# Routed expert loop: both weight blocks of a tile's expert copied at once into four buffers, and the choice of experts worked out in two parts of tiles

## Chip, cores, metric

The kernel runs on one core of one Trainium2 chip. The metric is the device time of one execution in microseconds (us). Engines are named as in the profile: PE is TensorE's matmuls, PEld its weight loads, DVE is VectorE, ACT is ScalarE, POOL is GpSimd, SP is SyncE (here only an issuer of DMAs).

## The reference, cut to what matters

The whole program is a two-layer network over x of 128 x 32 x 128 (4096 tokens of width 128). The change lies in the feed-forward part of layer 0, a mixture of 8 experts with two choices for each token:

```python
logits = x @ router_weight                  # x: 4096 x 128, 8 experts
probs = jax.nn.softmax(logits, axis=-1)
top_p, top_i = jax.lax.top_k(probs, 2)
top_p = top_p / jnp.sum(top_p, axis=-1, keepdims=True)
...                                         # an expert keeps its first cap choices, in token order
fc1 = jax.nn.gelu(jnp.einsum('ech,ehf->ecf', xt, moe_w1))      # moe_w1: 8 x 128 x 256
fc2 = jnp.einsum('ecf,efh->ech', fc1, moe_w2).reshape(T, H)    # moe_w2: 8 x 256 x 128
weighted = fc2 * padded_probs[:, None]
moe_out = jnp.zeros((N, H)).at[padded_tid].add(weighted)
return h1 + moe_out
```

The cap is 1280 choices per expert.

## The kernel before

The program is a row of stages, each with one instruction stream per engine and semaphores between them. The change touches `stage_experts_two`, which the profile shows from about 769 to 958 us. It holds 32 tiles of 128 tokens and treats them in two ways. Tiles 20 to 31 are **dense**: three blocks of four tiles, each through all 8 experts, with each expert's result added to the tokens with its share (zero if it isn't chosen). Tiles 0 to 19 are **routed**: each of their 2 x 2560 rows is stored to a row of a table in HBM that is sorted by expert, 48 tiles of 128 rows (`NS`), so that each tile has one expert.

In order, the stage does this:

1. **The choice** (DVE, lines 1848 to 1907): a chain of short instructions, each of which waits for the one before (`link`). It normalises the probabilities of all 32 tiles, finds the first and second expert (`first_of`), waits for two matmuls of PE that count the earlier tokens of each expert (`ranks`, lines 1733 and 1734), makes prefix sums over tiles, and from these the shares (`expert_shares`, semaphore `known`), the table rows of the first and second choices (`slots`, semaphore `slots_known`, one count for each choice), and the expert of each of the 48 tiles (`tile_expert`, `tiles_known`).
2. **The scatter** (POOL, line 1715): 40 indirect DMAs, one for each routed tile and choice, the first 20 after `slots_known` 1.
3. **Dense, early** (PE, ACT, DVE): meanwhile two of the three dense blocks. PE makes `h` (line 1739) and `y` (line 1749) of an expert, ACT the gelu between (line 1815), DVE adds the result (`take`, line 1924). The fourth `y` of PE waits for `known`, since its bank 7 is the one that the rank matmuls used.
4. **The routed loop** (48 tiles; the first and last 8 are written out, 32 run as four passes of a hardware loop with eight tiles in its body). SP loads a tile's rows from the table into one of 8 buffers (line 1692), and reloads a buffer when the store of its last tile's results has landed. PE transposes it (line 1767), ACT copies the transpose out of PSUM (line 1820), PE makes `slot_h` (line 1774), ACT the gelu (line 1830), PE makes `slot_y` (line 1783), DVE scales it by the token's share (`y_scale`, line 1936) into one of 4 buffers, and POOL stores it to HBM by an indirect DMA (line 1721). The tile's expert is known only in `tile_expert`, so an engine reads it into a register (`value_load`): DVE does so to copy `w1` of the expert into one of two buffers (`pick`, line 1931), PE does so to address `w2` in `slot_y`:

```python
e = pe.value_load(tile_expert[0:1, ts(t, 1)], min_val=0, max_val=E - 1)
pe.wait_ge(t_gelued, t + 1)
wait(pe, y_scaled, t - 1)
for c in range(NF):
    m = pe.matmul(pZ[slot % 2][:, 0:D], tg[slot % 2][:, c * P:(c + 1) * P],
                  w2[:, bass.ds(e * F + c * D, D)], start=(c == 0), stop=(c == NF - 1))
```

   The order on each engine is written by hand: for tile t, PE does transpose(t+1), slot_h(t), slot_y(t-1); ACT x_copy(t+1), gelu(t); DVE pick(t+1), y_scale(t-1); POOL store(t).
5. **Dense, late** on PE, ACT and DVE (the third block), during which the routed results come back from HBM and are added (`join`).

## Time and profile before

| what | value |
|---|---|
| three runs | 2177.77 us median, 2172.71 to 2177.92 |
| the profiled execution | 2173.39 us, span 2171.6 us |
| PE busy, PEld busy | 1991.1 us (92%), 1477.1 us (68%) |
| DVE, ACT, POOL busy | 1559.5, 1261.6, 1177.0 us |
| mean granted TensorE clock | 0.967 of full speed |
| this stage: the choice on DVE | 769.5 to 794.1 us |
| this stage: scatters on POOL | 792.5 to 842.9 us |
| this stage: early dense on PE | 769.5 to 834.3 us |
| this stage: routed loop on PE | 846.2 to 923.8 us |
| this stage: late dense on PE | 924.2 to 952.5 us |

Times inside the span are read from the timeline, which gives starts and durations of the instructions. The busy shares of the page are means over many stages; for this change the stretch from 769 to 924 us has to be read by itself.

### The profile page before, as it was taken

The page shows a single profiled execution, that of the slowest core. Times are in us where ns is not written, and L with a number is a line of the kernel's source. Part 1 is how long each engine was busy: PE and PEld are TensorE (multiplying, and loading weights), DVE is VectorE, ACT ScalarE, POOL GpSimd, SP SyncE. Part 2 cuts the span into 40 slices and gives each one's busy share as a digit, 9 for nine tenths or more (in the row PEclk, how much of TensorE's full clock was granted, in tenths as well). Part 3 has the DMA queues.
Part 4 walks back from the last instruction along what each step waited for, and adds up shares of the span by engine and source line. Part 5 has one row for each costly group of instructions (what it writes and reads, how often), then busy time and mean ns, then how long its engine had stood idle before and what let it go on. Part 6 is the DMA issues. An engine that isn't in the chain of part 4 may idle for free. (4 is left out here: it accounts for less than half of the span.)

```text
span 2171.6 us, 80082 instructions
## 1 busy us (share of the span) xinstructions
PE 1991.1 (92%) x26973; PEld 1477.1 (68%) x26974; DVE 1559.5 (72%) x5584; ACT 1261.6 (58%) x3636; POOL 1177.0 (54%) x1217
## 2 busy tenths in 40 slices
PE   8989999997999797869999999999789999979998
PEld 5567777774767665647777777777456666666897
DVE  6878888883777763458989898989666676654444
ACT  4555556554888533527777777777545555542332
POOL 2234433442888635636777777777266666634331
PEclk9999999997999988979999999999899999989999
DMA  6630000000000002220111111111220000000113
GB/s 216 215 126 0 0 0 0 0 1 1 1 0 0 1 20 63 81 80 26 38 36 37 37 41 39 40 36 40 95 107 0 0 0 0 0 1 29 39 49 98
DMA packets 48256, 86.63 MB, mean 40 GB/s; under 512 B 8624, under 2 KB 34224, under 8 KB 47408
## 3 DMA queue, kind: packets, MB, share of 16 engines
q1 hardware_dynamic: 43040, 74.84, 10.8%
...
## 5 line engine op out<-in xcount | busy, mean ns | idle before, releaser
L2554 ACT ACTIVATE xat_scores<-xat_scores,xat_least 128x257 f32<-128x257 f32 x512 | 258.3, 505 | 84.5 <-DVE xat_least L2695 84.5
L2695 DVE CUSTOM_DVE_ANT_0 xat_scores<-bank,xat_mask_b 128x257 f32<-128x257 f32 x512 | 202.8, 419 | 51.2 <-PE bank L2400 45.1
L1109 POOL TENSOR_TENSOR gqa_rnorm<-gqa_norm_min,gqa_minus_half 128x12 f32<-128x12 f32 x64 | 145.8, 2278 | 104.7 <-DVE gqa_norm_min L1186 104.7
L2456 PE MATMUL bank<-ident,xat_scores 128*128 128x128 f32 x1024 | 189.6, 288 | 0.2 <-DVE xat_p_T L2702 0.2
L753 POOL TENSOR_TENSOR lin_q_softmax<-lin_q_exp,lin_q_rsum 128x512 f32<-128x512 f32 x64 | 66.7, 1042 | 223.0 <-DVE lin_q_rsum L814 223.0
L2456 PEld LDWEIGHTS bank<-ident,xat_scores 128*128 128x128 f32 x1024 | 116.1, 142 | 81.8 <-issue 43.8
L1427 POOL TENSOR_TENSOR bat_scores<-bat_scores,bat_max 128x512 f32<-128x512 f32 x128 | 130.4, 1040 | 32.6 <-DVE bat_max L1459 32.6
L1459 DVE CUSTOM_DVE_ANT_0 bat_scores<-bank,bat_causal_add 128x128 f32<-128x128 f32 x512 | 110.7, 286 | 47.1 <-PE bank L1315 47.1
L631 PEld LDWEIGHTS bank<-lin_w_v_out,lin_z_T 128*128 128x128 f32 x1024 | 119.1, 191 | 22.0 <-issue 20.2
L631 PE MATMUL bank<-lin_w_v_out,lin_z_T 128*128 128x128 f32 x1024 | 131.2, 281 | 1.3 <-ACT lin_z_T L683 1.3
L2600 POOL TENSOR_TENSOR xat_p_rsum_wide<-xat_p_rsum,xat_head_of_row 128x128 f32<-128x128 f32 x128 | 51.1, 399 | 147.1 <-DVE xat_p_rsum L2708 147.1
L2567 ACT ACTIVATE xat_p_T<-bank 128x256 f32<-128x256 f32 x256 | 96.3, 377 | 49.0 <-PE bank L2456 41.5
L2702 DVE COPY xat_p_T<-bank 128x256 f32<-128x256 f32 x256 | 106.3, 415 | 0.3 <-PE bank L2456 0.2
L2400 PE MATMUL bank<-xat_k_cos,xat_q_blocks 32*128 32x257 f32 x1024 | 94.8, 431 | 7.4 <-DVE xat_least L2695 3.0
L2554 ACT ACTIVATION_READ_ACCUMULATOR xat_scores<-xat_scores,xat_least 128x1 f32 x512 | 97.5, 190 | 0.0
L1056 ACT ACTIVATE gqa_squares<-bank 128x512 f32<-128x512 f32 x64 | 38.2, 597 | 91.8 <-PE bank L919 91.7
L1382 ACT ACTIVATE bat_p_T<-bank 128x512 f32<-128x512 f32 x128 | 76.1, 594 | 24.8 <-PE bank L1323 24.8
L1323 PEld LDWEIGHTS bank<-ident,bat_scores 128*128 128x128 f32 x512 | 54.9, 142 | 50.9 <-ACT bat_scores L1377 25.3
L1323 PE MATMUL bank<-ident,bat_scores 128*128 128x128 f32 x512 | 77.4, 285 | 12.7 <-ACT bat_scores L1377 12.7
...
L704 ACT ACTIVATE lin_q_T<-bank 128x512 f32<-128x512 f32 x64 | 38.2, 597 | 79.8 <-PE bank L594 79.8
L2409 PE MATMUL bank<-xat_ctx_kept,xat_w_k 128*128 128x257 f32 x256 | 78.4, 388 | 6.4 <-POOL xat_ctx_kept L2617 6.4
...
## 6 DMA issues: line engine op xcount, KB each, us to landing
...
moe_slot_row<-moe_rows SPq DMA_DIRECT2D x48, 65.0 KB, 1.8
...
```

The lines of the kernel that those rows point to most:

```text
L631: m = pe.matmul(pY[:, 0:D], zT[slot][:, hd, :], wvo[:, hd // 2, hd % 2, :], start=(hd == 0), stop=(hd == H - 1))
L1109: pool.tensor_tensor(rn[h][:, :], sm[h][:, :], half_neg[:, :], ALU.pow).then_inc(rnorm, 1)
L1323: m = pe.transpose(pT[g % 2][:, i * P:(i + 1) * P], sx[g][:, i, :], k.ident[:, :])
L1427: pool.tensor_tensor(sx[g][:, :, :], sx[g][:, :, :], spread(mx[g][:, :], P), ALU.subtract).then_inc(s_shifted, 1)
L1459: dve.tensor_tensor_reduce(sx[g][:, i, :], pS[g][:, i * P:(i + 1) * P], cadd[:, :], 1.0, -BIG, ALU.add, ALU.max, mx[g][:, i:i + 1]).then_i ...
L2400: m = pe.matmul(pS[g][:, 0:J], qb[slot][r, part, j, :, :], keys[j % 2][r, :], start=(part == 0), stop=(part == 1))
L2409: pe.matmul(pK[:, 0:J], wk[:, :], ck[slot][:, j, :], start=True, stop=True).then_inc(k_made, 1)
L2456: m = pe.transpose(dst[:, c * P:(c + 1) * P], sx[j % 2][:, g, c * P:(c + 1) * P], k.ident[:, :])
L2554: act.activation(sx[j % 2][:, g, :], sx[j % 2][:, g, :], ACT.Exp, bias=mn[j % 2][g][:, 0:1], scale=-1.0, accum_out=sm[j % 2][:, g:g + 1]). ...
L2567: act.activation(pt[j % 2][g][:, :], unit_bank(*at)[:, 0:NC * P], ACT.Copy).then_inc(pa_copied, 1)
L2695: dve.tensor_tensor_reduce(sx[j % 2][:, g, :], pS[g][:, 0:J], mb[slot][:, j, :], 1.0, BIG, ALU.add, ALU.min, mn[j % 2][g][:, 0:1]).then_in ...
L2702: dve.tensor_copy(pt[j % 2][g][:, :], unit_bank(*at)[:, 0:NC * P]).then_inc(pd_copied, 1)
```

## The change

- `w1` and `w2` of an expert lie side by side in one array of 512 columns per expert (`wp`; one load of the same bytes instead of two).
- `pick` copies all 512 columns into one of **four** buffers, and waits for `slot_y` of three tiles before instead of `slot_h` of the last tile. `slot_y` takes `w2` from the same buffer: PE's `value_load` and its computed addresses go.
- The choice is worked out in two parts, tiles 0 to 19 (160 columns) and tiles 20 to 31 (96 columns): choose(0), share(0), choose(1), rank(0), the table rows of the first choice, share(1), rank(1), the rows of the second choice, the tiles' experts. A part has its own rank matmuls (in banks 6 and 7); a third matmul with a matrix of -1 takes the place of one subtraction on DVE. The limit and the share are made in one instruction. PE waits for `known` 1 before its third `y` and for `known` 2 before its fourth.
- `look` at the end of the stage and `LATE` are the same work written in another way.

```diff
-        we = [sb(f"picked_w1{i}", [P, F]) for i in range(2)]
+        we = [sb(f"picked_w{i}", [P, 2 * F]) for i in range(4)]
...
-        pR, pC = k.bank[7][:, 0:NT * E], k.bank[7][:, NT * E:2 * NT * E]
+        PARTS = ((0, NR), (NR, NT))
+        pR = [k.bank[6 + part][:, 0:(hi - lo) * E] for part, (lo, hi) in enumerate(PARTS)]
+        pC = [k.bank[6 + part][:, (hi - lo) * E:2 * (hi - lo) * E] for part, (lo, hi) in enumerate(PARTS)]
...
+            pool.memset(minus[:, :], -1.0).then_inc(ones_set, 1)
...
         def _(pe):
-            def ranks():
-                pe.wait_ge(ones_set, 1)
-                pe.wait_ge(sel_ready, 1)
-                pe.matmul(pR, low[:, :], sel[:, :, :], start=True, stop=True)
-                pe.matmul(pC, ones[:, :], sel[:, :, :], start=True, stop=True).then_inc(ranked, 1)
+            def ranks(part):
+                lo, hi = PARTS[part]
+                pe.wait_ge(ones_set, 2)
+                pe.wait_ge(sel_ready, part + 1)
+                pe.matmul(pR[part], low[:, :], sel[:, lo:hi, :], start=True, stop=False)
+                pe.matmul(pR[part], minus[:, :], sel[:, lo:hi, :], start=False, stop=True)
+                pe.matmul(pC[part], ones[:, :], sel[:, lo:hi, :], start=True, stop=True).then_inc(ranked, 1)
 
...
-                    pe.matmul(pH[e % 2][c][:, :], w1[:, e * F + c * P:e * F + (c + 1) * P], k.LT[:, ts(b, TB), :],
+                    pe.matmul(pH[e % 2][c][:, :], wp[:, 2 * e * F + c * P:2 * e * F + (c + 1) * P], k.LT[:, ts(b, TB), :],
...
                 pe.wait_ge(gelued, NF * n + NF)
                 wait(pe, added, TB * (n - BANKS + 1))
-                if n == BANKS - 1:
-                    pe.wait_ge(known, 1)
+                if BANKS - 2 <= n < BANKS:
+                    pe.wait_ge(known, n - BANKS + 3)
...
-                                      w2[:, (e * NF + c) * D:(e * NF + c + 1) * D], start=(c == 0), stop=(c == NF - 1))
+                                      wp[:, (2 * e + 1) * F + c * D:(2 * e + 1) * F + (c + 1) * D], start=(c == 0), stop=(c == NF - 1))
...
-                        if ranking and i == 0 and e == 2:
-                            ranks()
+                        if ranking and i == 0 and 1 <= e < 3:
+                            ranks(e - 1)
...
-                    m = pe.matmul(pT[slot % 2][:, c * P:(c + 1) * P], we[slot % 2][:, c * P:(c + 1) * P], xT[slot % 2][:, :],
+                    m = pe.matmul(pT[slot % 2][:, c * P:(c + 1) * P], we[slot % 4][:, c * P:(c + 1) * P], xT[slot % 2][:, :],
...
             def slot_y(t, slot):
-                e = pe.value_load(tile_expert[0:1, ts(t, 1)], min_val=0, max_val=E - 1)
                 pe.wait_ge(t_gelued, t + 1)
                 wait(pe, y_scaled, t - 1)
                 for c in range(NF):
                     m = pe.matmul(pZ[slot % 2][:, 0:D], tg[slot % 2][:, c * P:(c + 1) * P],
-                                  w2[:, bass.ds(e * F + c * D, D)], start=(c == 0), stop=(c == NF - 1))
+                                  we[slot % 4][:, F + c * D:F + (c + 1) * D], start=(c == 0), stop=(c == NF - 1))
                 m.then_inc(ty_made, 1)
...
+            def choose(lo, hi):
+                p, o0, o1, c = pr[:, lo:hi, :], oh[0][:, lo:hi, :], oh[1][:, lo:hi, :], k.COMB[:, lo:hi, :]
+                a, b, sums, t = top[:, lo:hi], top2[:, lo:hi], tot[:, lo:hi], tmp[:, lo:hi, :]
+                link(dve.tensor_reduce(sums, p, AX, ALU.add))
+                link(dve.reciprocal(sums, sums))
+                link(dve.tensor_tensor(p, p, spread(sums, E), ALU.mult))
+                link(dve.tensor_reduce(a, p, AX, ALU.max))
+                link(dve.tensor_copy(sums, a))
+                first_of(dve, link, t, o0, p, a, down[:, :])
+                link(dve.scalar_tensor_tensor(out=c, in0=o0, scalar=-2.0, in1=p, op0=ALU.mult, op1=ALU.add))
+                link(dve.tensor_reduce(b, c, AX, ALU.max))
+                link(dve.tensor_tensor(sums, sums, b, ALU.add))
+                first_of(dve, link, t, o1, c, b, down[:, :])
+                dve.tensor_tensor(sel[:, lo:hi, :], o0, o1, ALU.add).then_inc(sel_ready, 1)
+
+            def share(part, lo, hi):
+                dve.wait_ge(sel_ready, part + 1)
+                link(dve.reciprocal(tot[:, lo:hi], tot[:, lo:hi]))
+                link(dve.tensor_tensor(pr[:, lo:hi, :], pr[:, lo:hi, :], spread(tot[:, lo:hi], E), ALU.mult))
+                link(dve.tensor_tensor(pr[:, lo:hi, :], pr[:, lo:hi, :], sel[:, lo:hi, :], ALU.mult))
+
+            def rank(part, lo, hi, before):
+                n = hi - lo
+                dve.wait_ge(ranked, part + 1)
+                link(dve.tensor_copy(acc[0][:, lo:hi, :], pC[part].rearrange("p (t e) -> p t e", e=E)))
+                if before is not None:
+                    link(dve.tensor_tensor(acc[0][:, lo, :], acc[0][:, lo, :], before, ALU.add))
+                d, a = 1, 0
+                while d < n:
+                    link(dve.tensor_copy(acc[1 - a][:, lo:lo + d, :], acc[a][:, lo:lo + d, :]))
+                    link(dve.tensor_tensor(acc[1 - a][:, lo + d:hi, :], acc[a][:, lo + d:hi, :], acc[a][:, lo:hi - d, :],
+                                           ALU.add))
+                    d, a = 2 * d, 1 - a
+                link(dve.tensor_tensor(tmp[:, lo:hi, :], acc[a][:, lo:hi, :], pR[part].rearrange("p (t e) -> p t e", e=E),
+                                       ALU.add))
+                dve.scalar_tensor_tensor(out=k.COMB[:, lo:hi, 0:E], in0=tmp[:, lo:hi, :], scalar=float(CAP),
+                                         in1=pr[:, lo:hi, :], op0=ALU.is_lt, op1=ALU.mult).then_inc(known, 1)
+                dve.wait_ge(known, part + 1)
+                return acc[a][:, hi - 1, :]
+
+            def slot_numbers(c):
+                link(dve.tensor_tensor(picks[:, :, :], spot[:, :, :], oh[c][:, 0:NR, :], ALU.mult))
+                link(dve.tensor_reduce(spots[c][:, :], picks[:, :, :], AX, ALU.add))
+                link(dve.tensor_tensor(picks[:, :, :], k.COMB[:, 0:NR, :], oh[c][:, 0:NR, :], ALU.mult))
+                link(dve.tensor_reduce(kept[c][:, :, SHARE], picks[:, :, :], AX, ALU.add))
+                dve.tensor_copy(slots[c][:, :], spots[c][:, :]).then_inc(slots_known, 1)
...
-            link(dve.tensor_reduce(tot[:, :], pr[:, :, :], AX, ALU.add))
-            link(dve.reciprocal(tot[:, :], tot[:, :]))
...
-            first_of(dve, link, tmp[:, :, :], oh[1][:, :, :], k.COMB[:, :, :], top2[:, :], down[:, :])
-            dve.tensor_tensor(sel[:, :, :], oh[0][:, :, :], oh[1][:, :, :], ALU.add).then_inc(sel_ready, 1)
-            dve.wait_ge(sel_ready, 1)
-            link(dve.reciprocal(tot[:, :], tot[:, :]))
-            link(dve.tensor_tensor(pr[:, :, :], pr[:, :, :], spread(tot[:, :], E), ALU.mult))
-            link(dve.tensor_tensor(pr[:, :, :], pr[:, :, :], sel[:, :, :], ALU.mult))
-
-            dve.wait_ge(ranked, 1)
-            in_tile = pC.rearrange("p (t e) -> p t e", e=E)
-            link(dve.tensor_copy(acc[0][:, :, :], in_tile))
-            d, a = 1, 0
-            while d < NT:
-                link(dve.tensor_copy(acc[1 - a][:, 0:d, :], acc[a][:, 0:d, :]))
-                link(dve.tensor_tensor(acc[1 - a][:, d:, :], acc[a][:, d:, :], acc[a][:, 0:NT - d, :], ALU.add))
-                d, a = 2 * d, 1 - a
-            link(dve.tensor_tensor(tmp[:, :, :], acc[a][:, :, :], in_tile, ALU.subtract))
-            link(dve.tensor_tensor(tmp[:, :, :], tmp[:, :, :], pR.rearrange("p (t e) -> p t e", e=E),
-                                   ALU.add))
...
-            link(dve.tensor_scalar(need[:, :], acc[a][:, NR - 1, :], 1.0 / P, None, ALU.mult))
+            choose(*PARTS[0])
+            share(0, *PARTS[0])
+            choose(*PARTS[1])
+            counts = rank(0, *PARTS[0], None)
+
+            link(dve.tensor_scalar(need[:, :], counts, 1.0 / P, None, ALU.mult))
...
-            link(dve.tensor_scalar(tmp[:, :, :], tmp[:, :, :], float(CAP), None, ALU.is_lt))
-            dve.tensor_tensor(k.COMB[:, :, 0:E], pr[:, :, :], tmp[:, :, :], ALU.mult).then_inc(known, 1)
-            dve.wait_ge(known, 1)
-            for c in range(2):
-                link(dve.tensor_tensor(picks[:, :, :], spot[:, :, :], oh[c][:, 0:NR, :], ALU.mult))
-                link(dve.tensor_reduce(spots[c][:, :], picks[:, :, :], AX, ALU.add))
-                link(dve.tensor_tensor(picks[:, :, :], k.COMB[:, 0:NR, :], oh[c][:, 0:NR, :], ALU.mult))
-                link(dve.tensor_reduce(kept[c][:, :, SHARE], picks[:, :, :], AX, ALU.add))
-                dve.tensor_copy(slots[c][:, :], spots[c][:, :]).then_inc(slots_known, 1)
+            slot_numbers(0)
+            share(1, *PARTS[1])
+            rank(1, *PARTS[1], counts)
+            slot_numbers(1)
...
             def pick(t, slot):
                 e = dve.value_load(tile_expert[0:1, ts(t, 1)], min_val=0, max_val=E - 1)
-                wait(dve, th_made, t - 1)
-                dve.tensor_copy(we[slot % 2][:, :], w1[:, ts(e, F)]).then_inc(picked, 1)
+                wait(dve, ty_made, t - 3)
+                dve.tensor_copy(we[slot % 4][:, :], wp[:, bass.ds(e * 2 * F, 2 * F)]).then_inc(picked, 1)
...
-            moe_w = [eb("moe_w1", [P, 8 * 256]), eb("moe_w2", [P, 8 * 2 * D])]
+            moe_w = eb("moe_w", [P, 8 * 512])
...
+    o["moe_w"] = np.concatenate([g["L0_ffn_moe_w1"].transpose(1, 0, 2),
+                                 g["L0_ffn_moe_w2"].reshape(8, 2, P, D).transpose(2, 0, 1, 3).reshape(P, 8, -1)],
+                                axis=2).reshape(P, -1)
```

On PE, in the routed loop (written-out part, third and fourth tile; `bank` is PSUM, `moe_w` the experts' weights, `moe_picked_w` the copy of the tile's expert). Before:

```order
L1767 MATMUL bank<-ident,moe_slot_row 128x128
L1774 MATMUL bank<-moe_slot_xT,moe_picked_w 128x128 x2
L1779 TENSOR_LOAD moe_tile_expert
L1779 ISA x2
L1783 ISA
L1783 MATMUL bank<-moe_w,moe_slot_gelu 128x128
L1783 ISA
L1783 MATMUL bank<-moe_w,moe_slot_gelu 128x128
L1767 MATMUL bank<-ident,moe_slot_row 128x128
L1774 MATMUL bank<-moe_slot_xT,moe_picked_w 128x128 x2
```

With the change:

```order
L1773 MATMUL bank<-ident,moe_slot_row 128x128
L1780 MATMUL bank<-moe_slot_xT,moe_picked_w 128x128 x2
L1788 MATMUL bank<-moe_picked_w,moe_slot_gelu 128x128 x2
L1773 MATMUL bank<-ident,moe_slot_row 128x128
L1780 MATMUL bank<-moe_slot_xT,moe_picked_w 128x128 x2
L1788 MATMUL bank<-moe_picked_w,moe_slot_gelu 128x128 x2
```

The register load (TENSOR_LOAD) and the four instructions that set addresses are gone, and slot_y reads moe_picked_w.

On DVE, the same place: scaling of one tile, then the pick for the tile after the next. Before:

```order
L1936 TENSOR_SCALAR moe_slot_y<-bank,moe_slot_row 128x128
L1929 TENSOR_LOAD moe_tile_expert
L1929 ISA x2
L1931 ISA
L1931 COPY moe_picked_w<-moe_w 128x256
L1936 TENSOR_SCALAR moe_slot_y<-bank,moe_slot_row 128x128
```

With the change:

```order
L1958 TENSOR_SCALAR moe_slot_y<-bank,moe_slot_row 128x128
L1951 TENSOR_LOAD moe_tile_expert
L1951 ISA x2
L1953 ISA
L1953 COPY moe_picked_w<-moe_w 128x512
L1958 TENSOR_SCALAR moe_slot_y<-bank,moe_slot_row 128x128
```

The register load stays here; the copy has 512 columns instead of 256.

On DVE, the end of the chain that the scatter waits for, from the last prefix sum to the first choice's rows. Before:

```order
L1892 TENSOR_SCALAR moe_tokens_of<-moe_tokens_of 128x8
L1893 TENSOR_TENSOR moe_spot<-moe_tmp,moe_tokens_of 128x160
L1895 TENSOR_SCALAR moe_tmp<-moe_tmp 128x256
L1896 TENSOR_TENSOR expert_shares<-moe_probs,moe_tmp 128x256
L1899 TENSOR_TENSOR moe_picked_spot<-moe_spot,moe_onehot 128x160
L1900 TENSOR_REDUCE moe_slot_float<-moe_picked_spot 128x20
L1901 TENSOR_TENSOR moe_picked_spot<-expert_shares,moe_onehot 128x160
L1902 TENSOR_REDUCE moe_rows_kept<-moe_picked_spot 128x20
L1903 CAST moe_slot<-moe_slot_float 128x20
```

With the change, up to the beginning of the second part's prefix sums:

```order
L1919 TENSOR_SCALAR moe_tokens_of<-moe_tokens_of 128x8
L1920 TENSOR_TENSOR moe_spot<-moe_tmp,moe_tokens_of 128x160
L1894 TENSOR_TENSOR moe_picked_spot<-moe_spot,moe_onehot 128x160
L1895 TENSOR_REDUCE moe_slot_float<-moe_picked_spot 128x20
L1896 TENSOR_TENSOR moe_picked_spot<-expert_shares,moe_onehot 128x160
L1897 TENSOR_REDUCE moe_rows_kept<-moe_picked_spot 128x20
L1898 CAST moe_slot<-moe_slot_float 128x20
L1870 RECIPROCAL moe_total<-moe_total 128x12
L1871 TENSOR_TENSOR moe_probs<-moe_probs,moe_total 128x96
L1872 TENSOR_TENSOR moe_probs<-moe_probs,moe_selected 128x96
L1877 COPY moe_prefix<-bank 128x96
```

The two 256-column instructions between moe_spot and the rows are gone from here; the second part's shares and ranks stand between the first and the second choice's rows.

## Rows read from the trace of the kernel before

**Rows 1.** Waits, 800 to 960 us: engine, line, waited for; total us, times, longest.

```profile
PEld bank L1783 <- issue: 19.0, 46, 0.6
...
PE bank L1767 <- DMA moe_slot_row<-moe_rows: 11.9, 1, 11.9
```

**Rows 2.** Windows: busy us (x instructions) per engine, PEclk, DMA share, GB/s.

```profile
850.00:852.00 2.00, 2.00 (x11) 2.00 (x11) 0.70 (x2) 0.84 (x2) 0.42 (x1) 0.50 0.00 0
```

**Rows 3.** Timeline of the routed loop: start us, us, engine, line, operation, [idle before].

```profile
891.84 0.53 PEld L1774 LDWEIGHTS bank<-moe_slot_xT,moe_picked_w 128*128 128x128 f32 x4
...
892.04 0.35 DVE L1936 TENSOR_SCALAR moe_slot_y<-bank,moe_slot_row 128x128 f32<-128x128 f32 x1 [0.30 <-PE bank L1783]
...
892.84 0.71 PE L1783 MATMUL bank<-moe_w,moe_slot_gelu 128*128 x4 [0.28 <-issue]
892.89 0.29 DVE L1931 COPY moe_picked_w<-moe_w 128x256 f32 x1 [0.50 <-PE bank L1774]
893.18 0.96 POOL L1721 DMA_INDIRECT moe_results<-moe_slot_y,moe_slot_row  x1 [0.50 <-issue]
...
893.59 0.35 DVE L1936 TENSOR_SCALAR moe_slot_y<-bank,moe_slot_row 128x128 f32<-128x128 f32 x1 [0.40 <-PE bank L1783]
```

**Rows 4.** Timeline, GpSimd: first and last issue of a pass of eight, next pass.

```profile
888.70 0.96 POOL L1721 DMA_INDIRECT moe_results<-moe_slot_y,moe_slot_row  x1 [1.35 <-DVE moe_slot_y L1936]
...
899.28 0.96 POOL L1721 DMA_INDIRECT moe_results<-moe_slot_y,moe_slot_row  x1 [0.64 <-issue]
901.72 0.96 POOL L1721 DMA_INDIRECT moe_results<-moe_slot_y,moe_slot_row  x1 [1.48 <-DVE moe_slot_y L1936]
```

**Rows 5.** DMA issues, 844 to 928 us: KB each, median us from issue to landing.

```profile
moe_slot_row<-moe_rows SPq DMA_DIRECT2D x48, 65.0 KB, 1.8
moe_results<-moe_slot_y,moe_slot_row POOLq DMA_INDIRECT x48, 2.2
```

**Rows 6.** Timeline, VectorE: the last eight tiles, written out.

```profile
912.67 0.35 DVE L1936 TENSOR_SCALAR moe_slot_y<-bank,moe_slot_row 128x128 f32<-128x128 f32 x1 [0.31 <-PE bank L1783]
...
916.60 0.33 DVE L1931 COPY moe_picked_w<-moe_w 128x256 f32 x1 [0.78 <-PE bank L1774]
916.91 0.35 DVE L1936 TENSOR_SCALAR moe_slot_y<-bank,moe_slot_row 128x128 f32<-128x128 f32 x1
...
921.44 0.35 DVE L1936 TENSOR_SCALAR moe_slot_y<-bank,moe_slot_row 128x128 f32<-128x128 f32 x1 [0.46 <-PE bank L1783]
```

**Rows 7.** Groups by form: the later routed stage's copy of 1024 columns.

```profile
L2224 DVE COPY slt_w<-expert_w 128x1024 f32 x40 | 27.8, 694 | 12.8 <-issue 12.5
```

**Rows 8.** Timelines: a copy on VectorE beside an indirect issue on GpSimd, twice.

```profile
860.38 0.29 DVE L1931 COPY moe_picked_w<-moe_w 128x256 f32 x1 [0.68 <-PE bank L1774]
...
860.49 1.02 POOL L1721 DMA_INDIRECT moe_results<-moe_slot_y,moe_slot_row  x1 [0.48 <-issue]
...
886.40 0.96 POOL L1721 DMA_INDIRECT moe_results<-moe_slot_y,moe_slot_row  x1 [0.61 <-issue]
886.49 0.29 DVE L1931 COPY moe_picked_w<-moe_w 128x256 f32 x1 [0.88 <-PE bank L1774]
```

**Rows 9.** Timeline, VectorE, the choice: first step, wait, 160 columns, slots, dense sums; POOL.

```profile
771.21 0.42 DVE L1851 TENSOR_REDUCE moe_total<-moe_probs 128x32 f32<-128x256 f32 x1 [0.83 <-ACT moe_probs L1833]
...
781.51 0.43 DVE L1871 COPY moe_prefix<-bank 128x256 f32<-128x256 f32 x1 [1.79 <-PE bank L1734]
...
789.91 0.33 DVE L1899 TENSOR_TENSOR moe_picked_spot<-moe_spot,moe_onehot 128x160 f32<-128x160 f32 x1
...
791.34 0.18 DVE L1903 CAST moe_slot<-moe_slot_float 128x20 uint32<-128x20 f32 x1
...
794.21 5.26 DVE L1924 SCALAR_TENSOR_TENSOR X<-bank,expert_shares,X 128x128 f32<-128x128 f32 x20
...
792.49 1.22 POOL L1715 DMA_INDIRECT moe_rows<-moe_rows_kept,moe_slot  x1 [22.52 <-DVE moe_slot L1903]
```

**Rows 10.** Timelines of TensorE and its loads; then the group of scatters on GpSimd.

```profile
790.02 3.10 PE L1749 MATMUL bank<-moe_w,moe_gelu 128*128 128x128 f32 x16 [3.40 <-DVE expert_shares L1896]
...
830.59 3.54 PEld L1749 LDWEIGHTS bank<-moe_w,moe_gelu 128*128 128x128 f32 x31 [0.24 <-issue]
...
L1715 POOL DMA_INDIRECT moe_rows<-moe_rows_kept,moe_slot x40 | 38.5, 964 | 34.4 <-DVE moe_slot L1903 22.5 <-issue 11.9
```

32 lines of the change are left out of this document (11 added, 21 removed).

## Prediction

> **What bounds the kernel now.** The page says that PE is busy for 92% of the span, so I looked for the stretches of the changed stage in which PE waits. The table of waits gives two [rows 1]: once 11.9 us for the first loaded rows of the routed loop, and 46 times a mean of 19.0/46 = 0.41 us before the weight loads of slot_y (L1783), put down to "issue", so to nothing that another engine did. The rest of the stage's PE time is dense work, which the change doesn't touch.
>
> The first wait says that the early dense part is covered: the scatter on POOL is longer. It is 40 indirect issues of 0.964 us with 11.9/39 = 0.30 us between them, 1.27 us each, and back to back from the moment the first choice's rows are known [rows 10]. So the path into the loop is: choice on DVE, scatter, load. Cover for everything on PE and DVE beside it: 11.9 us.
>
> The second is in the routed loop. The timeline shows one tile [rows 3]: y_scale at 892.04, pick at 892.89, the next y_scale at 893.59, 0.04 us after slot_y's end (892.84 + 0.71). A full pass of eight tiles takes 901.72 - 888.70 = 13.02 us, of which the step over the loop's branch is 901.72 - 899.28 = 2.44, and the seven others are 10.58/7 = 1.51 us [rows 4]. PE's own need is less: in the dense part 31 loads go in 3.54 us, one each 0.112 us [rows 10], so the nine passes of a tile (one transpose, four each for slot_h and slot_y) are 1.01 us. The gap makes up the difference: 1.01 + 0.41, and some 0.1 for the hand-overs. PE sets today's pitch, with DVE close behind it: y_scale to pick is 0.85 us though y_scale lasts 0.35, since pick's register load takes that long from the issue of the instruction before it.
>
> **Part 1: PE's register load goes.** PE falls from about 1.5 to 1.01 us for a tile and no longer sets the pitch. Three others are next, and I price each.
>
> - DVE. y_scale to pick 0.85 [rows 3]. The copy has 512 columns instead of 256. The trace has no such copy; its bounds are 0.29 us for 256 columns [rows 3] and 0.694 for 1024 [rows 7]. Both lie on one line, 0.157 + columns x 0.00052, which gives **0.42 us**. Once, where DVE was late, y_scale began 0.31 after a 256-column copy (916.91 - 916.60) [rows 6], so nothing is lost between the two: period 0.85 + 0.42 = **1.27 us**.
> - The loop over both engines: pick(t) done, slot_h 0.07 later, slot_y 0.45 after that (four passes), its end 0.71 later, y_scale 0.04 later: 1.27; then 0.85 + 0.42 to the pick of the tile after the next. That is 2.54 us for two tiles, 1.27 for one. With four buffers pick's own wait is for slot_y of three tiles before, whose y_scale it has passed already, so it costs nothing.
> - POOL. 1.27 us for an issue when it never waits [rows 10]. The longer copy now reaches into its issue: POOL starts 1.14 after y_scale (893.18 - 892.04), the copy will run from 0.85 to 1.27. The nearest case is a copy that ran 0.18 us into an issue, which lasted 1.02 instead of 0.96 [rows 8]. So 1.27 + 0.06 = **1.33**; the lower bound is 1.27, the upper 1.27 + 0.42 = 1.69 if the whole copy is added (a rival below).
>
> I take **1.32** for a step inside a pass and leave the branch step's extra 0.93 as it is, since every engine pays it. A hardware pass: 7 x (1.51 - 1.32) + 0.19 = 1.5 us less; four of them 6.1. The last eight tiles are written out and go at (921.44 - 912.67)/6 = 1.46 [rows 6]; with 1.27 for the six, 1.1 less, and the last two, which have no pick and only PE's gap to lose, 0.7 less. In the first eight, PE is at half its clock, granted 0.50 [rows 2], until 852 us: there the passes take twice as long, there is no gap to win, and only the five steps after it gain, 0.1 each: 0.5. Sum for the loop: **8.4 us**, between 3.5 (a step of 1.43) and 10.5 (a step of 1.27 and half of the branch's extra hidden).
>
> The buffers of table rows come next after these: a store must land before its buffer is reloaded. At a step of 1.32, eight steps are 10.6 us; from a tile's transpose to its y_scale go two steps and 1.3 (3.9 with the wait for DVE), 1.14 to POOL's start, 2.2 for the store's landing and 1.8 for the reload's, by the medians [rows 5], and 0.3 for the reissue, 9.4 in all. About 1 us of room: it does not bind, but a late landing would show.
>
> **Part 2: the choice in two parts.** What counts is when the first choice's rows are known, today 771.21 to 791.52 [rows 9], 20.3 us. A step of the chain on 256 columns is 0.42 + 0.035 us; on 160 columns 0.33 + 0.03 [rows 9]; 96 columns I put on the same line at 0.29. The choosing has 14 such steps and about 0.8 of small ones: instead of 7.2 us it is 5.8 for 20 tiles and 4.7 for 12, **+3.3**. share on 160 columns: -0.25. The wait of 1.79 for the rank matmuls [rows 9] goes, since the first part's run under choose(1): **-1.8**. The prefix sums of 20 tiles with the share made at their end, 3.8 against 4.5: -0.7. The two 256-column steps before the rows go: -0.8. Sum **-0.3 us**. So the split buys the scatter almost nothing; bounds -1.0 and +0.7, by 0.03 us on each of the 28 halves.
>
> It moves PE's and DVE's other work later. The second part's shares are known at 791.2 + 0.9 (share) + 3.0 (rank) = 795.1, and the dense sums on DVE begin after that, the rows of choice 1 (1.5, as 789.91 to 791.34 [rows 9]) and the tiles' experts (two steps on 384 columns, 0.59 each on the same line, and a small one, 1.4), at 798.0 instead of 794.2 [rows 9]. PE's fourth y, which began at 790.02 after a wait of 3.40 [rows 10], begins at 795.2. The early dense part ends some 5.2 us later, at 839.5, DVE's last sum at 840.7, its first two picks by 842.5; the loop's first transpose is at 846. The extra matmuls (first part 6 passes, second part 6, against 4) and POOL's second memset are hidden too. Price 0, with 11.9 - 5.2 = 6.7 us of cover left; without it each us would be a us. A later end also changes how long PE is idle before the loop: granted 0.50 at 850 to 852 [rows 2] may end sooner or later, at most 2 us either way.
>
> Weights in one array: same bytes, same passes, loaded long before: 0.
>
> **Sum.** -8.4 - 0.3 = **-8.7 us**. The profiled execution was 2173.39 us (span 2171.6), so 2164.7 for such a one. The median of the runs is 4.4 us above it, at 2177.77, and one of three is at 2172.71; from the median I get **2169.0 us**, 0.4% less. A measurement of this kernel can tell about 0.3%, 6.5 us, from no change.
>
> **Rivals.**
>
> - **A: another pitch binds at about 1.42.** The reload of row buffers (room 1 us, with single landings far above the median), or hand-overs that cost more than in rows 3, as the sum 1.01 + 0.41 falls 0.09 short of the 1.51 seen. Then the loop gives 44 x 0.09 = 4 us, 2173.5. For: three cycles at 1.27 to 1.33 disturb one another. Against: with median landings a row buffer has 1 us of room. Chance 0.14.
> - **B: the gap before slot_y isn't the register load** but the semaphores that stay. Then PE stays at 1.5, and the change doesn't do what it says: 0 to 1 us, about 2177. Against: slot_h, which also waits for two other engines, has no idle time before its loads (the row at 891.84 [rows 3] lists none). Chance 0.07.
> - **C: slower, by the port between DVE and GpSimd.** If a fast copy and an indirect issue shut each other out, each tile pays both in a row: 1.27 + 0.42 = 1.69 against 1.51, 44 x 0.18 = 8 us more, 2185.5. It decides from 0.24 us of stretch on each issue. Against: the copy at 886.49 lies wholly inside the issue that began at 886.40, and they last 0.29 and 0.96, as alone [rows 8]; the one stretch seen is 0.06. The Trainium skill states this exclusion as a rule (SBUF — State Buffer, "SBUF: two separate sides"): while DVE runs an fp32 copy from SBUF to SBUF in its two-port mode, GpSimd can't write the descriptors of its DMAs. By that rule the trace should show issues or copies lengthened by up to a whole partner, and the copy inside the issue speaks against it. Chance 0.05.
>
> **Numbers.** The forecast (a step of 1.27 to 1.38) has 0.74. The range: from 2162 (10.5 us won, and a median 5 us lower within the group, like the run of 2172.71) to 2177 (case A with little won). C and the tails stay outside, about 0.15. Faster by over 0.3%: 0.66 from the forecast (it misses the bound if the step is over 1.36) and 0.02 from A: 0.68. Within 0.3%: 0.26. Slower: 0.06, C and a little of B.
>
> **What would show it.** Right: no idle time of PE before slot_y; y_scale to y_scale 1.27 to 1.35 and a pass of eight 11.2 to 11.7 us; the copy 0.42; indirect issues of 1.02; loop from first transpose to last y_scale 70 us instead of 78; first scatter within 1 us of 792.49 [rows 9]; PE's longest wait in the early dense part about 5 us and its wait before the loop some 6.5. Wrong: a step over 1.42, an issue over 1.1, PE waiting for landed rows inside the loop, or the loop starting later than 847.

## The result, and the profile after

| what | before | changed |
|---|---|---|
| median, five runs each | 2174.02 us (2172.71 to 2177.92) | 2160.29 us (2157.38 to 2163.48) |
| profiled execution, span | 2173.39, 2171.6 us | 2159.83, 2157.6 us |
| routed stage (first step of the choice to the next stage's first step on DVE) | 189.5 us | 179.1 us |
| everything else in the span | 1982.1 us | 1978.5 us |

The ratio is 0.9933 with a 95% interval of 0.9917 to 0.9949: faster by 13.7 us of the medians, where 8.7 were forecast. The time is 1.7 us below the forecast range. The direction is as forecast, and 10.4 of the 13.7 us are in the stage that was changed.

In the waits of the changed kernel, 760 to 945 us, the line that set the old pitch is gone, and GpSimd's issues stand in its place:

```profile
DVE moe_picked_w L1953 <- issue: 25.0, 47, 1.0
...
POOL moe_results L1725 <- issue: 16.6, 45, 0.7
...
PEld bank L1780 <- issue: 10.0, 28, 0.6
POOL moe_results L1725 <- DVE moe_slot_y L1958: 9.9, 3, 8.7
...
PE bank L1773 <- DMA moe_slot_row<-moe_rows: 5.9, 3, 5.4
```

slot_y (L1788 now) has no line of its own where the kernel before had 19.0 us in 46 waits [rows 1]. By this table POOL waited for y_scale only 3 times, and 8.7 of those 9.9 us are its wait for the first tile; but its waits under "issue" hold more of the same, as the starts below show. TensorE's wait before the loop is now 5.4 us instead of 11.9. The timeline of GpSimd in the loop (start, duration, idle before it), from the last two steps of one pass over the branch and through the next pass:

```profile
878.85 0.96 POOL L1725 DMA_INDIRECT moe_results<-moe_slot_y,moe_slot_row  x1 [0.32 <-issue]
880.52 1.01 POOL L1725 DMA_INDIRECT moe_results<-moe_slot_y,moe_slot_row  x1 [0.71 <-issue]
882.06 0.98 POOL L1725 DMA_INDIRECT moe_results<-moe_slot_y,moe_slot_row  x1 [0.53 <-issue]
883.35 0.95 POOL L1725 DMA_INDIRECT moe_results<-moe_slot_y,moe_slot_row  x1 [0.30 <-issue]
...
889.86 0.96 POOL L1725 DMA_INDIRECT moe_results<-moe_slot_y,moe_slot_row  x1 [0.31 <-issue]
891.52 1.01 POOL L1725 DMA_INDIRECT moe_results<-moe_slot_y,moe_slot_row  x1 [0.70 <-issue]
```

A pass is 891.52 - 880.52 = 11.00 us (13.02 before [rows 4]). Its seven inner steps take 889.86 - 880.52 = 9.34, 1.334 each, and the step over the branch 1.66 (2.44 before). VectorE in the same stretch:

```profile
886.15 0.35 DVE L1958 TENSOR_SCALAR moe_slot_y<-bank,moe_slot_row 128x128 f32<-128x128 f32 x1 [0.22 <-PE bank L1788]
887.02 0.43 DVE L1953 COPY moe_picked_w<-moe_w 128x512 f32 x1 [0.52 <-issue]
887.37 0.34 DVE L1958 TENSOR_SCALAR moe_slot_y<-bank,moe_slot_row 128x128 f32<-128x128 f32 x1
888.29 0.43 DVE L1953 COPY moe_picked_w<-moe_w 128x512 f32 x1 [0.58 <-issue]
888.72 0.35 DVE L1958 TENSOR_SCALAR moe_slot_y<-bank,moe_slot_row 128x128 f32<-128x128 f32 x1
890.04 0.43 DVE L1953 COPY moe_picked_w<-moe_w 128x512 f32 x1 [0.97 <-issue]
890.38 0.34 DVE L1958 TENSOR_SCALAR moe_slot_y<-bank,moe_slot_row 128x128 f32<-128x128 f32 x1
```

The copy takes 0.43 us, y_scale often follows with no idle time, and the register load before each copy now shows as 0.5 us of "issue" (0.97 over the branch). The first transpose is at 842.97 (846.24 before), the last y_scale ends at 910.99 (924.17), so the loop takes 68.0 us instead of 77.9.

How far POOL is behind VectorE can be read from the starts. In no kernel here does an issue begin sooner than 0.79 us after the end of its tile's y_scale, and in the kernel before 47 of the 48 begin 0.79 to 0.81 us after it: POOL waited for nearly every tile. In the changed kernel 25 of the 48 still do. The issue over the branch is one of them: y_scale ends at 890.38 + 0.34 = 890.72, and the issue begins at 891.52. So POOL now sets the pitch in about half of the steps, with VectorE level with it, and the extra that is left over the branch is VectorE's (0.97 us before the copy instead of 0.52 to 0.58).

The choice begins at 768.39 in this execution. What PE waits for, in its timeline (the second part's ranks, the third and the fourth y, the loop's first transpose):

```profile
780.01 0.43 PE L1738 MATMUL bank<-moe_selected,earlier_rows 128*128 128x96 f32 x2 [1.21 <-DVE moe_selected L1866]
...
783.62 2.02 PE L1755 MATMUL bank<-moe_w,moe_gelu 128*128 128x128 f32 x16 [0.98 <-DVE expert_shares L1888]
...
792.38 3.75 PE L1755 MATMUL bank<-moe_w,moe_gelu 128*128 128x128 f32 x16 [5.02 <-DVE expert_shares L1888]
...
842.97 0.83 PE L1773 MATMUL bank<-ident,moe_slot_row 128*128 128x128 f32 x2 [5.40 <-DMA moe_slot_row<-moe_rows]
```

The slots of the first choice are known at 788.20, 19.8 us after the start (20.3 before), so 0.5 us are won there in this pair of executions. The old choice takes 20.2 us in loop_only and 19.8 in before_unrolled, two kernels that leave it alone (the wait for its rank matmuls is 1.70 and 1.32 us there, 1.79 before), so the gain is anything from 0 to 0.5 us. PE's third y waits 0.98 and its fourth 5.02 us, all of it under the cover that is left.

### The profile page after: what moved, and what is told of

It reads as the page before. It is cut to its first block and busy times, and to the rows that moved or that the text cites. A ratio compares the mean times of both kernels' runs of the same rounds, so it can differ in the third digit from the quotient of the medians.

```text
span 2157.6 us, 79866 instructions
## 1 busy us (share of the span) xinstructions
PE 1989.1 (92%) x26981; PEld 1475.4 (68%) x26982; DVE 1567.2 (73%) x5614; ACT 1263.4 (59%) x3636; POOL 1178.0 (55%) x1218
## 3 DMA queue, kind: packets, MB, share of 16 engines
q1 hardware_dynamic: 42896, 74.84, 10.8%
## 5 line engine op out<-in xcount | busy, mean ns | idle before, releaser
L2477 PE MATMUL bank<-ident,xat_scores 128*128 128x128 f32 x1024 | 189.7, 288 | 0.2 <-DVE xat_p_T L2723 0.2
L631 PEld LDWEIGHTS bank<-lin_w_v_out,lin_z_T 128*128 128x128 f32 x1024 | 119.1, 191 | 22.0 <-issue 20.2
L1323 PEld LDWEIGHTS bank<-ident,bat_scores 128*128 128x128 f32 x512 | 54.9, 142 | 50.9 <-ACT bat_scores L1377 25.3
L1323 PE MATMUL bank<-ident,bat_scores 128*128 128x128 f32 x512 | 77.5, 285 | 12.8 <-ACT bat_scores L1377 12.8
## 6 DMA issues: line engine op xcount, KB each, us to landing
moe_rows<-in_moe_empty SPq DMA_DIRECT2D x1, 3120.0 KB, 15.4
```

Source lines behind the costliest of these rows:

```text
L631: m = pe.matmul(pY[:, 0:D], zT[slot][:, hd, :], wvo[:, hd // 2, hd % 2, :], start=(hd == 0), stop=(hd == H - 1))
L1323: m = pe.transpose(pT[g % 2][:, i * P:(i + 1) * P], sx[g][:, i, :], k.ident[:, :])
L2477: m = pe.transpose(dst[:, c * P:(c + 1) * P], sx[j % 2][:, g, c * P:(c + 1) * P], k.ident[:, :])
```

## Experiments

Throughout, "stage" is the routed stage as in the table, in one profiled execution, and "loop" goes from the first transpose to the end of the last y_scale. "Theory 1" in the expectation of static_pick is the prediction's.

### The two halves by themselves

Only the loop's change, with the old choice:

```diff
-        PARTS = ((0, NR), (NR, NT))
...
-            def ranks(part):
+            def ranks():
...
-                if BANKS - 2 <= n < BANKS:
-                    pe.wait_ge(known, n - BANKS + 3)
+                if n == BANKS - 1:
+                    pe.wait_ge(known, 1)
...
-            choose(*PARTS[0])
-            share(0, *PARTS[0])
-            choose(*PARTS[1])
-            counts = rank(0, *PARTS[0], None)
...
```

> The changed kernel with the choice of experts as before (one part of 32 tiles); only the loop's part of the change. If the loop carries the gain: from first transpose to the end of the last y_scale 68 us, as with the whole change (before: 77.9), the early dense part ends as before, some 12 us ahead of the loop, and the time is within 1 us of the whole change's, 10 us under before. If the split choice carries a part (the rows of the first choice 3 us or more later here): 7 us under before or less.

Measured: 2159.21 us, ratio 0.9935 (0.9913 to 0.9958). Stage 179.2 us, loop 67.5. PE waits 12.2 us for the first rows, as before the change:

```profile
PE bank L1768 <- DMA moe_slot_row<-moe_rows: 12.8, 4, 12.2
```

Only the choice in two parts, with the old loop:

```diff
+        PARTS = ((0, NR), (NR, NT))
...
+            choose(*PARTS[0])
+            share(0, *PARTS[0])
+            choose(*PARTS[1])
+            counts = rank(0, *PARTS[0], None)
...
```

> The kernel before with the choice in two parts; only that part of the change. By my sum it starts the scatter 0.3 us earlier (0.5 us in the changed kernel's trace) and delays the early dense part by 3 to 5 us under cover: loop 77.9 us long, time within 1 us of before. Rival, that the split is worth 4 us as the measured difference of 14 us is larger than the 10 us found in this stage: 3 to 5 us faster than before.

Measured: 2171.72 us, ratio 0.9991 (0.9979 to 1.0002); stage 188.8 us, 0.7 below before, loop 77.8. So the loop's part carries the whole gain that a measurement can tell. The split is worth at most 0.5 to 0.7 us in the stage, and in the total it can't be told from nothing.

### What set the old pitch: the register load on PE

Pick copies w1 alone here, 256 columns, into four buffers, and PE loads its register again:

```diff
-        we = [sb(f"picked_w{i}", [P, 2 * F]) for i in range(4)]
+        we = [sb(f"picked_w{i}", [P, F]) for i in range(4)]
...
             def slot_y(t, slot):
+                e = pe.value_load(tile_expert[0:1, ts(t, 1)], min_val=0, max_val=E - 1)
...
-                                  we[slot % 4][:, F + c * D:F + (c + 1) * D], start=(c == 0), stop=(c == NF - 1))
+                                  wp[:, bass.ds(e * 2 * F + F + c * D, D)], start=(c == 0), stop=(c == NF - 1))
```

> The changed kernel, but pick copies w1 alone (256 columns, into four buffers) and slot_y reads w2 at an address from a register that PE loads, as before. If PE's register load is what set the old pitch: the loop takes 76 to 78 us, PE idle 0.4 us before every slot_y. If the buffers and pick's weaker wait gave the gain: 70 us or less.

Measured: 2168.88 us (one run), loop 78.6 us, stage 189.7. The gap is back, with its old size, though the four buffers are there:

```profile
PEld bank L1789 <- issue: 19.5, 45, 0.5
```

Rival B falls: the gap is the register load (0.43 us each), not the semaphores. Four buffers alone win nothing. The single run's total lies 4.7 us below the median of before although its stage is not shorter; why a total is no measure for half a per cent here is said under the forecast.

### What the four buffers are for

```diff
-        we = [sb(f"picked_w{i}", [P, 2 * F]) for i in range(4)]
+        we = [sb(f"picked_w{i}", [P, 2 * F]) for i in range(2)]
...
-                wait(dve, ty_made, t - 3)
+                wait(dve, ty_made, t - 1)
```

> The changed kernel with two buffers for the 512 columns instead of four; pick must then wait for slot_y of the tile two before. By the cycle slot_y end, hand-over 0.04, copy 0.43, hand-over 0.07, slot_h 0.45, slot_y to its end 0.71, a step is 1.7 us and the loop 80 us or more: slower than before by 2 to 6 us. If the buffers don't matter (DVE's or GpSimd's own pace is all): 68 to 70 us.

Measured: 2186.30 us (one run), loop 90.8 us, 13 us longer than before the change; the total is 12.8 us above that of before, where 2 to 6 were expected. The new waits of VectorE's pick and TensorE:

```profile
DVE moe_picked_w L1953 <- PE bank L1788: 59.6, 46, 7.1
...
PEld bank L1780 <- ACT moe_slot_xT L1825: 31.8, 40, 1.0
```

With two buffers, pick has to wait until slot_y of the tile before last has read the second block, and then the copy and slot_h follow in a row (the register is loaded ahead of this wait, in pick's order of instructions). The step is 1.85 us (four passes in 59.05). It is the four buffers that make the gain possible: without them the copy of both blocks costs more than PE's register load did.

### What sets the new pitch: DVE's register load or POOL's issue

In the next two kernels the routed tiles all take the weights of expert 0. First the register load alone goes, and the copy stays:

```diff
-                e = dve.value_load(tile_expert[0:1, ts(t, 1)], min_val=0, max_val=E - 1)
...
-                dve.tensor_copy(we[slot % 4][:, :], wp[:, bass.ds(e * 2 * F, 2 * F)]).then_inc(picked, 1)
+                dve.tensor_copy(we[slot % 4][:, :], wp[:, 0:2 * F]).then_inc(picked, 1)
```

> The changed kernel, but pick always copies the weights of expert 0 and DVE loads no register: the routed tiles' results are those of expert 0. Theory 1, GpSimd's issues of the stores set the new pace (1.27 us each and what copies add): the loop stays at 64 to 68 us, indirect issues back to back with 0.30 us between. Theory 2, DVE sets it (0.85 + 0.43): DVE now needs 0.8 us for a tile, the loop falls to PE's 1.0 us for a tile, 50 to 56 us.

Then the copy goes as well, and PE reads the same columns of `wp` in place:

```diff
             def pick(t, slot):
-                e = dve.value_load(tile_expert[0:1, ts(t, 1)], min_val=0, max_val=E - 1)
-                wait(dve, ty_made, t - 3)
-                dve.tensor_copy(we[slot % 4][:, :], wp[:, bass.ds(e * 2 * F, 2 * F)]).then_inc(picked, 1)
+                dve.sem_inc(picked, 1)
```

> As static_pick, but without any copy: PE reads the weights of expert 0 in place; the routed tiles' results are those of expert 0. If the fast copies stretch GpSimd's issues: every issue lasts 0.96 us here, steps are 1.27 us, and the loop is 1 to 2 us shorter than with static_pick. If the copies cost GpSimd nothing: same length as static_pick.

Measured: loops of 65.2 us (static_pick) and 67.2 us (no_pick). The totals, 2246.02 and 2249.92, belong to another stage and are taken up below. With no copy at all, the timeline of GpSimd over two passes reads:

```profile
878.35 0.96 POOL L1725 DMA_INDIRECT moe_results<-moe_slot_y,moe_slot_row  x1 [0.30 <-DVE moe_slot_y L1956]
...
888.44 0.95 POOL L1725 DMA_INDIRECT moe_results<-moe_slot_y,moe_slot_row  x1 [0.30 <-DVE moe_slot_y L1956]
...
898.53 0.95 POOL L1725 DMA_INDIRECT moe_results<-moe_slot_y,moe_slot_row  x1 [0.31 <-DVE moe_slot_y L1956]
```

Eight steps take 10.09 us, 1.26 each, with **nothing extra over the branch**, though all engines still run the hardware loop. This is POOL alone: 0.96 for an issue, 0.30 between two (the rows name y_scale, but it had ended 1.1 to 2 us before in all of these steps). So the pass of 11.00 us in the changed kernel is 10.1 of POOL, some 0.5 in which the seven inner steps are longer (1.334 for 1.26), and 0.4 over the branch. Of the 0.5, about 0.1 are longer issues and 0.4 are waits for a late y_scale, above all in the first step behind the branch (1.54). With static_pick the passes are 10.1 to 10.5, and no issue in them begins less than 1.08 us after y_scale's end: without its register load VectorE has a reserve. But the load alone doesn't cost the 0.9 either: with the load kept and the branch gone (after_unrolled, below) two of the four passes take 10.1 and 10.3 us. It takes both, and removing either wins most of it back.

no_pick's loop is not the shortest, although its passes are. It loses at the ends: its first eight steps take 11.74 us (static_pick 11.25, changed kernel 11.31) and its last seven 11.37 (9.47, 8.96). There a row buffer's reload comes late:

```profile
PE bank L1773 <- DMA moe_slot_row<-moe_rows: 10.0, 5, 5.2
PEld bank L1773 <- DMA moe_slot_row<-moe_rows: 8.3, 16, 1.8
```

That is rival A's mechanism, the eight row buffers: 1.6 us once at each end here. It isn't peculiar to this kernel. static_pick has single waits of this kind too (up to 1.2 us), and so has after_unrolled (up to 0.9); in the changed kernel the longest inside the loop is 0.3.

### The hardware loop's branch

In the kernel before the change, the four middle passes of PE, DVE, ACT, POOL and SP written out:

```diff
-            with eng.Fori(0, NS // WAYS - 2) as i:
+            for i in range(NS // WAYS - 2):
...
-            with sp.Fori(0, NS // WAYS - 1) as i:
+            for i in range(NS // WAYS - 1):
```

> The kernel before with all 48 tiles of the routed loop written out. The prediction let the hardware loop's branch cost 0.93 us at each of five or so seams. If that price is right here: loop 73 to 75 us instead of 77.9, and steps of 1.46. If the branch cost is something else (the first tiles after it wait for rows): 77 us or more.

Measured: 2172.16 us (one run); loop 71.8 us (77.9 before), stage 182.9. That is more than the 3 to 5 us expected. The total hardly moves, because the rest of the span happened to take 1987.4 us in this execution, the longest of all whose cross-attention stage is undisturbed. The same edit in the changed kernel:

> The changed kernel with all 48 tiles written out. In its trace a seam adds 0.3 us between two of GpSimd's issues, not 0.93. If GpSimd's backlog hides the rest of a branch: loop 65.5 to 67.5 us instead of 68.0, time 0 to 2 us under the changed kernel. If the branch still costs 0.9 at each seam: 63.5 us, 4 us less.

Measured: loop 65.5 us (68.0), stage 176.6, so writing the passes out wins 2.6 us there, against 6.1 in the kernel before. The four passes take 10.3, 10.8, 10.1 and 10.8 us; the two longer ones hold the waits for landed rows named above. But the total is 2243.10 us, ratio 1.0325 (1.0304 to 1.0345), 83 us **slower** than the changed kernel. The time is in the cross-attention stage, which neither edit touches: 682 us for 598.

### The choice ordered by who needs it first

```diff
-            choose(*PARTS[1])
...
             slot_numbers(0)
+            choose(*PARTS[1])
             share(1, *PARTS[1])
...
-                        if ranking and i == 0 and 1 <= e < 3:
-                            ranks(e - 1)
+                        if ranking and i == 0 and e in (1, 3):
+                            ranks(e // 2)
```

> The changed kernel with the choosing for tiles 20 to 31 moved behind the table rows of the first choice (the second part's rank matmuls one expert later). Those 4.6 us then lie behind the start of the scatter: scatter and loop start 4 to 4.5 us earlier, DVE's dense sums at the same time as now, so the early dense part ends at the very moment when the loop can start; 3.5 to 4.5 us under the changed kernel. If the early dense part was the true gate, or PE's wait for the moved matmuls delays it: 0 to 2 us.

Measured: 2154.51 us, ratio 0.9913 (0.9898 to 0.9927), so 5.8 us less than the changed kernel, where 3.5 to 4.5 were expected; stage 173.6. The second part's choosing, 4.7 us, now comes behind the slots of the first. The timelines of VectorE (the first step of the choice, then the slots) and TensorE (the second part's ranks):

```profile
770.89 0.32 DVE L1856 TENSOR_REDUCE moe_total<-moe_probs 128x20 f32<-128x160 f32 x1 [0.83 <-ACT moe_probs L1838]
...
786.15 0.18 DVE L1898 CAST moe_slot<-moe_slot_float 128x20 uint32<-128x20 f32 x1
...
791.09 0.71 PE L1738 MATMUL bank<-moe_selected,earlier_rows 128*128 128x96 f32 x2 [6.28 <-DVE moe_selected L1866]
```

15.4 us to the slots instead of 19.8. PE pays with a wait of 6.28 us, which is under the scatter's cover, but now nearly all of it: PE waits for landed rows no longer than 1.8 us in this kernel. 4.4 of the 5.5 us of the stage are these earlier slots. The other 1.1 are in the loop (66.9 us), 0.8 of them in its first eight steps, which TensorE begins at half its clock in both kernels. Here it waited 1.81 us before the loop and is granted the full clock (1.00 in the windows) again some 4 us after the loop's start at 841.0; in the changed kernel it waited 5.40 us, and it takes some 6.5 us from the start at 843.0. In windows (busy us per engine, PEclk, DMA share, GB/s), late_part and then the changed kernel:

```profile
844.00:846.00 2.00, 2.00 (x15) 1.98 (x14) 0.56 (x2) 1.13 (x3) 0.00 (x0) 0.73 0.00 0
```

```profile
848.00:850.00 2.00, 2.00 (x13) 2.00 (x13) 0.84 (x3) 0.97 (x3) 0.96 (x1) 0.64 0.09 33
```

That the clock is the whole reason for the 0.8 us isn't shown by itself.

### Why an untouched stage became slower

after_unrolled, static_pick and no_pick all lose 84 to 93 us in cross-attention, the others nothing. In the waits of VectorE there (930 to 1700 us), after_unrolled and then the changed kernel:

```profile
DVE xat_scores L2716 <- issue: 66.1, 35, 3.4
DVE xat_scores L2716 <- PE bank L2421: 54.9, 76, 1.6
```

```profile
DVE xat_scores L2716 <- PE bank L2421: 45.3, 76, 1.6
...
DVE xat_scores L2716 <- issue: 4.2, 8, 0.7
```

and in the queues' part of after_unrolled's page (queue, kind: packets, MB, share):

```profile
q14 instruction: 108, 0.88, 0.1%
```

It is 41 packets and 0.34 MB in the changed kernel. The additional fetches lie inside the stage: between 1050 and 1480 us after_unrolled has the following row (the changed kernel has no such row at all), and VectorE's timeline there shows two long waits in 13 of the 14 turns of the stage's hardware loop, some 42 us apart:

```profile
q14 instruction: 53, 0.43, 0.3%
```

```profile
1098.86 0.43 DVE L2716 CUSTOM_DVE_ANT_0 xat_scores<-bank,xat_mask_b 128x257 f32<-128x257 f32 x1 [3.28 <-issue]
1100.87 0.43 DVE L2716 CUSTOM_DVE_ANT_0 xat_scores<-bank,xat_mask_b 128x257 f32<-128x257 f32 x1 [1.58 <-issue]
...
1140.47 0.43 DVE L2716 CUSTOM_DVE_ANT_0 xat_scores<-bank,xat_mask_b 128x257 f32<-128x257 f32 x1 [3.08 <-issue]
```

So VectorE stands still 13 times, at one place in a turn, for some 5 us, while instructions are fetched again, about five packets a turn. The other waits of that row, 0.7 us and less, are there in the changed kernel too. Two kernels tested whether the place of VectorE's code decides. In both, one-column memsets (`TOTAL` of them, 127 or 136) are added on VectorE among the dense sums, where it sits idle:

```diff
+        more = sb("more", [P, TOTAL])
...
                                              op0=ALU.mult, op1=ALU.add).then_inc(added, 1)
+                if 5 <= n < 15:
+                    for m in range(TOTAL * (n - 5) // 10, TOTAL * (n - 4) // 10):
+                        dve.memset(more[:, m:m + 1], 0.0)
```

The changed kernel with 127 of them:

> The changed kernel with 127 one-column memsets more on DVE, 12 or 13 behind each of ten groups of dense sums, where DVE sits idle 2.4 us before the next group; nothing else differs, and the loop stays a hardware loop with its register loads. They put the code of the cross-attention loop 127 instructions further on in DVE's program, to where it stands in the changed kernel with its routed loop written out (instruction 1526 of DVE's program; 1399 in the changed kernel). Theory of placement (DVE's instructions are fetched again at every turn of the cross-attention loop when its code stands in an unlucky place): the cross-attention stage grows from 598 to about 680 us, the DVE waits 'issue' before xat_scores from 4 us to 65, queue q14 from 41 packets to about 108, and the total comes to 2240 us or so. Rival (it is the written-out loop itself, or the missing register load, that leaves something behind which slows the later stage): the stage stays at 598 us, q14 near 41 packets, and the total at 2158 to 2164. The moe stage itself stays at 179 us by both.

Measured: 2164.60 us (2155.01 to 2166.11), ratio 0.9957 (0.9942 to 0.9972), cross-attention 598.0 us, q14 43 packets. So the count of VectorE's instructions ahead of the loop is **not** what decides; the rule that I had drawn from six kernels falls.

> The changed kernel with part 1 of the choice moved behind the slot numbers of part 0 (the run late_part: 2154.5 us), the middle passes of the routed loop written out, and 136 one-column memsets on DVE among the dense sums, so that the cross-attention loop stands at instruction 1662 of DVE's program. The loops that ran well stood at 1367, 1399 and 1496, those that ran badly at 1276, 1302 and 1526; seen modulo 256 that is 87, 119 and 216 against 252, 22 and 246, and 1662 is 126, inside the good stretch. Seen modulo 512 it is 343, 375 and 472 against 252, 278 and 502, and 1662 is 126, on no known side, rather the bad one. Theory of placement with a period of 256: the cross-attention stage takes 598 us, the routed loop 65 us instead of 67, and the total is 2151 to 2153 us, the best of all. With a period of 512, or if the written-out loop is itself the cause: the stage takes 680 us and the total is about 2235.

Measured: 2149.43 us (2147.03 to 2151.82), ratio 0.9890 (0.9873 to 0.9906), the fastest of all; cross-attention 595.6 us, loop 65.0, stage 171.5. This alone doesn't say what cured the stage, so the same kernel ran without its memsets:

> The last run's kernel without its 136 memsets, so part 1 of the choice moved and the middle passes of the routed loop written out. It tells whether the memsets (more code on DVE ahead of the cross-attention stage) or the moved part kept that stage at 596 us. Theory 1 (where DVE's code lies decides, though not by the simple count of instructions that the run after_more refuted; this kernel's DVE program has the loop at 1526 as the slow one had): the cross-attention stage takes about 680 us, its 'issue' waits before xat_scores 65 us, total about 2235. Theory 2 (the order of the choice's parts decides, or the slow stage needs both the written-out loop and the early part): 596 us, total 2147 to 2152.

Measured: 2240.56 us, ratio 1.0310 (1.0288 to 1.0332), cross-attention 687.2 us. VectorE's waits there, without and then with the memsets:

```profile
DVE xat_scores L2716 <- issue: 68.1, 36, 3.4
```

```profile
DVE xat_scores L2720 <- issue: 4.2, 8, 0.7
```

The stage itself (171.9 and 171.5 us) is the same. So **136 instructions that do nothing make this kernel 91 us faster** (instruction packets 44 instead of 108). The size of VectorE's code ahead of a later hardware loop can decide whether that loop is fetched again in every turn; this much is shown, as the two kernels differ in nothing but the memsets and the tile that they write. Which lengths are bad, and why a kernel with the hardware loop kept and 127 instructions more is well, stays open. The idle time on "issue", 66 to 75 us in the four slow kernels for 4 in the others, also leaves 20 to 25 of the 84 to 93 us to what follows from it on the other engines, which was not followed up.

## Why the prediction was right or wrong

- **The bound of the old loop: right.** With the register load back on PE the loop is back at 78.6 us (pe_load_kept).
- **The inner step: right in number, in part by luck.** Forecast 1.32, measured 1.334. The copy was put at 0.42 and took 0.43, and POOL was the right engine to look at: taking VectorE's load away (static_pick) wins only 2.8 us more of the loop. But the 0.06 over POOL's own 1.27 was put down to issues that the copies stretch, and in the pass above they are stretched by 0.02 on average (0.03 over all 48: 0.985 us for 0.957 in no_pick). The other 0.05 is waiting for y_scale, most of it in the step behind the branch. Where the passes are written out, with the same copies, most steps take 1.26 to 1.27 us.
- **"leave the branch step's extra 0.93 as it is, since every engine pays it": wrong, and the step of the working that failed.** The step over the branch takes 0.33 us more than the others in the changed kernel and nothing more in no_pick, whose engines run the same hardware loop. What decided was the register loads: with PE's load kept (pe_load_kept) the three steps between passes take 2.39, 2.36 and 2.32 us, with it gone 1.61, 1.67 and 1.66 (2.33, 2.30 and 2.44 before), and with VectorE's gone too (static_pick) POOL has no idle time over its usual 0.30 there. I read this so: an engine that is early hides its branch behind the engine that sets the pitch, and with a register load on PE and on DVE neither was early. Some 2.1 us were won in those three steps, of which the forecast had 0.6, and the eighth tile, where the hardware loop is entered, has another such step (2.07 before, 1.62 after).
- **The first eight and the last eight: off in size, in opposite ways.** From POOL's first issue to its ninth, 12.77 us became 11.31: 1.5 us for a forecast 0.5. The clock was granted 0.50 for the first 6 us or so in both, so that isn't the difference; the steps after it won 0.1 to 0.45 each where 0.1 was put, 0.86 of it in the last two, around the entry of the hardware loop. From the 41st issue to the last, 9.96 became 8.96: 1.0 for a forecast 1.8, since the last two steps were already 1.34 and 1.27 us before, POOL's own pace, and there was none of the forecast 0.7 to win in them. A pass of 11.00 us is shorter than the 11.2 to 11.7 named as the sign of being right. The four middle passes gave 50.9 - 43.9 = 7.0 for a forecast 6.1. The loop as a whole: 9.9 for 8.4.
- **The split choice: right, as far as it can be told.** 0 to 0.5 us for a forecast 0.3. The cover was priced at 6.7 us left, and 5.4 are left; PE's long wait was 5.0 us for "about 5".
- **The median it was set against: 3.8 us too high.** The forecast took 8.7 us off 2177.77, the median of three. With two more runs the same kernel's median is 2174.02, and five other groups of 7 to 13 runs gave 2173.5 to 2175.2. Of the 8.7 us between the forecast 2169.0 and the measured 2160.3, 3.8 are this median, 1.7 are the stage (10.4 us won for 8.7), and 3.3 lie outside it. So the branch's price is a fault in the working, but it didn't carry the result out of the range: an exact sum for the stage would have given 2167.4, and with the better median 2163.6, both inside it. It took all three together. The low end of the range, 2162, allowed for such a median together with 10.5 us won, and not for time outside the stage, which the sum leaves out without a reason.
- **What stays open: 3.3 us outside the stage.** The medians differ by 13.7 us, the stage by 10.4. Outside the stage the span was 1982.1 us before and 1978.5 after, but over the ten kernels whose cross-attention stage is undisturbed it is anything from 1973.8 to 1987.4 in a single execution. 2.8 of the 3.6 us lie ahead of the stage: the choice begins at 771.21 before and at 768.39 after, and in all fourteen traces between 767.5 and 772.8. I found no mechanism that ties it to the change, and the interval of the ratio, 11 to 18 us, begins close to the stage's 10.4.
- **Rival A** (a pitch of 1.42 by late row buffers) fell: three waits for landed rows, 5.4 of 5.9 us the first. Its mechanism exists, and shows as single waits of 0.9 to 1.6 us in no_pick, static_pick and after_unrolled, whose steps are shorter. **Rival B** fell with pe_load_kept. **Rival C** (the port): the longest issue in the changed loop took 1.15 us, 0.19 over the 0.96 of one alone, and the mean is longer by 0.03; the copies stayed at 0.43 (with the passes written out, every second one took 0.50). It would have had to be 0.24 on each. The Trainium skill's rule (SBUF — State Buffer, "SBUF: two separate sides"), by which such a copy and GpSimd's descriptor writes exclude each other, would have the issue wait for up to a whole copy, 0.43 us. The trace doesn't agree with that size in this loop: twice in the middle passes a copy of 0.43 us lay wholly inside an issue, and both issues took 0.96.
